# A graph-attention kernel: its general-path flag drawn in two steps, the last tile's stores on SP and GpSimd, and a last pass of 12 chunks

## The chip, the cores and the metric

The kernel runs on one core of one Trainium2 chip. A core has TensorE (PE, matrix products), VectorE (DVE), ScalarE (ACT), GpSimd (POOL) and SyncE (SP); each has its own instruction stream, they meet at semaphores, and 16 DMA engines move data between HBM and the on-chip memory. DMAs are issued here by SP, ACT and POOL. The metric is the time of one execution on the device in microseconds, the median of several.

## The reference, cut to what matters

One graph-attention layer over 4096 nodes with 128 features, then a residual and a layer norm:

```python
s_i = emb @ attn[:d]; s_j = emb @ attn[d:]          # emb is x, 4096 x 128
e = leaky_relu(s_i + s_j.T, negative_slope=0.2)
e = e + where(adj > 0, 0.0, -1e9)                   # adj is 4096 x 4096 int32
alpha = softmax(e, axis=1)
x = layernorm(x + alpha @ emb, axis=-1)
```

## The kernel before

**Main part.** The 4096 rows are 32 tiles of 128 rows, in 8 blocks of K = 4 tiles. The columns are 32 chunks of 128. For block n and chunk c, DVE makes one tile `weights` (128 x 512, line 674) out of row factors, column factors and the mask; PE then multiplies it, tile by tile, with `xj[:, c, 0:129]` (line 807; the 129th column gives the denominator) and sums over the chunks in four PSUM banks, one for each tile of the block. There are W_SLOTS = 12 buffers for `weights`: DVE may write chunk c once PE has used chunk c - 12 (semaphore `weights_used`). The adjacency comes in 32 pieces of 2 MB, half by SP's and half by ACT's DMAs; ACT turns them into bytes, DVE transposes those.

**The last pass.** In blocks 0 to 6 PE does the four tiles of each chunk in turn. In the last block it does this for the first CHUNKS - LAST chunks (LAST is 8) and then finishes tile after tile: 8 chunks of tile 0, 8 of tile 1, and so on (lines 827 to 835). After each of tiles 0 to 2 it raises `tile_summed`; the end of tile 3 is seen through `weights_used`.

**After the sums.** Tile 0 to tile 3 mean here the four tiles of the last block. They are handled in FINAL_GROUPS: tiles 0 and 1 together, tile 2, tile 3. For each group DVE clips the denominator (`denominators`, line 607), inverts it (`invert`, 613), forms y = sum/denominator + x (`add_x`, 619), and takes mean and variance (640 and 643). Group 0 is normalised by POOL (lines 324 to 331, reciprocal root) and ACT (465) and stored by POOL (4 DMAs of 32 KB, line 257 in `store_last`). For tiles 2 and 3 ACT takes the root of the variance (473), DVE inverts it (648) and normalises (651), raising `last_out_ready` to 1 and to 2; SP stores the partitions of quadrants 0 and 1 and ACT those of quadrants 2 and 3, two DMAs of 16 KB each for each tile (also `store_last`). SP and ACT issue tile 2's before tile 3's.

**The flag.** The fast computation holds only if no inverse of a denominator was very large. `worst` gathers the largest inverses (`largest_inverse`, line 625, after every block), DVE reduces it over its columns (666), PE turns the result into a row (839), DVE reduces the row (708) and compares it with MOST (710). The result is `again`, a number that every engine but POOL loads (`value_load`) to decide whether it jumps over the general path, a long piece of code of its own (lines 281 to 290, 487 and on, 713 and on, 842 and on). With the inputs used here it is 0, and all jump.

**The end.** Each engine goes to one last barrier (line 81, where the block of engine programs ends): a DRAIN, then a semaphore that POOL collects from all others before it lets them go. POOL gets there after it has waited for the landing of its own stores (`early_stored`), SP after its and ACT's stores (`last_stored`).

Of the kernel before, what the change touches and what calls it, by code (L numbers as in the profile page):

```python
# [9 lines left out]
def gat_kernel(nc: bass.Bass, x: bass.AP, adj: bass.AP, attn: bass.AP, out: bass.AP):  # L10
    fp32 = mybir.dt.float32
# [7 lines left out]
    P = 128  # L19
# [32 lines left out]
    LAST = 8  # L52
# [9 lines left out]
    MOST = 1e28  # L62
# [18 lines left out]
    with ExitStack() as ctx:  # L81
# [38 lines left out]
        worst = sb("worst", [P, T + 2], fp32)  # L120
# [69 lines left out]
        early_stored = sem("early_stored")  # L190
        last_stored = sem("last_stored")
# [6 lines left out]
        worst_turned = sem("worst_turned")  # L198
# [68 lines left out]
        @block.sync  # L267
        def _(sp):

            sp.dma_start(attn_row_in[:], attn[:, :].rearrange("d o -> o d")).then_inc(attn_loaded, 16)  # L270
            for part in range(X_PARTS):
                load_x(sp, LOW_HALF, part)
            for g in range(ALL_PIECES):
                load_piece(sp, LOW_HALF, g)


            for g in range(EARLY, len(FINAL_GROUPS)):
                sp.wait_ge(last_out_ready, g - EARLY + 1)
                for q in LOW_HALF:
                    store_last(sp, g, q, last_stored)  # L280


            sp.wait_ge(again_ready, 1)
            with sp.If(sp.value_load(again[0:1, 0:1], min_val=0, max_val=1) > 0):
                sp.wait_ge(stored, 16 * Q * NORM_GROUPS)
                sp.wait_ge(early_stored, 16 * Q * EARLY)
                sp.wait_ge(last_stored, 16 * Q * (len(FINAL_GROUPS) - EARLY))
                sp.dma_start(xi[:], xi_v).then_inc(inputs_again, 16)
                sp.dma_start(attn_col, attn[D:2 * D, :]).then_inc(inputs_again, 16)
                sp.dma_start(attn_row, attn[0:D, :].rearrange("d o -> o d").broadcast_to([P, D])).then_inc(inputs_again, 16)  # L290
                with sp.Fori(0, TILES) as t:
                    sp.wait_ge(adj_rows_free, t + 1)
                    sp.dma_start(adj_rows, adj[bass.ds(t * P, P), :]).then_inc(adj_rows_loaded, 16)
            sp.wait_ge(last_stored, 16 * Q * (len(FINAL_GROUPS) - EARLY))

        @block.gpsimd
        def _(pool):
# [34 lines left out]
            for g in range(EARLY):  # L332
                pool.wait_ge(early_out_ready, g + 1)
                for q in range(Q):
                    store_last(pool, g, q, early_stored)
            pool.wait_ge(early_stored, 16 * Q * EARLY)

        @block.scalar
        def _(act):
# [148 lines left out]
            with act.If(act.value_load(again[0:1, 0:1], min_val=0, max_val=1) > 0):  # L488
# [28 lines left out]
        def _(dve):  # L517
# [118 lines left out]
            def mean_and_variance(g):  # L636
                tiles = range(FINAL_GROUPS[g].start, FINAL_GROUPS[g].stop)
                for t in tiles:
                    dve.wait_ge(y_ready, FINAL + t + 1)
                    nc.vector.bn_stats(half_moments[:, t, :], tile(FINAL + t)).then_inc(half_moments_ready, 1)  # L640
                for t in tiles:
                    dve.wait_ge(half_moments_ready, t + 1)
                    nc.vector.bn_aggr(moments[:, t, :], half_moments[:, t, :]).then_inc(moments_ready, 1)  # L643
# [11 lines left out]
            def final_residual(n):  # L655

                for g in range(len(FINAL_GROUPS) + 1):
                    if g < len(FINAL_GROUPS):
                        denominators(n, g)
                        invert(n, g)  # L660
                        add_x(n, g)
                        mean_and_variance(g)
                    else:
                        largest_inverse(n)
                        dve.wait_ge(worst_ready, n + 2)
                        nc.vector.reduce_max(worst[:, T:T + 1], worst[:, 0:T], X).then_inc(worst_found, 1)
                    if g > EARLY:
                        last_normalise(g - 1)
# [45 lines left out]
            with dve.If(dve.value_load(again[0:1, 0:1], min_val=0, max_val=1) > 0):  # L714
# [41 lines left out]
        def _(pe):  # L756
# [81 lines left out]
            pe.wait_ge(worst_found, 1)  # L838
            nc.tensor.transpose(banks[0][0:1, 0:P], worst[:, T:T + 1], ident[:]).then_inc(worst_turned, 1)
# [3 lines left out]
            with pe.If(pe.value_load(again[0:1, 0:1], min_val=0, max_val=1) > 0):  # L843
# [51 lines left out]
```

## Time and profile before

| | us |
|---|---|
| median of 3 runs (lowest to highest) | 260.94 (260.23 to 261.37) |
| the profiled execution, its own time | 259.07 |
| its span (first to last instruction of the core) | 257.3 |
| outside the span, worked out | 1.8 |
| PE busy, DVE busy, ACT busy, POOL busy | 245.0, 235.3, 167.3, 37.4 |
| granted TensorE clock, mean | 0.994 |

The profile page gives busy time and shares over the whole span; the change touches only its last few microseconds, so that the view in order of time (start, duration, engine, line, tiles, count, and in brackets the idle time before and what ended it) is the one to read. The suffix q (PEldq, POOLq, SPq) stands for an engine's sequencer: branches, drains, register loads and DMA issues, which are not counted as busy. Such instructions are found by asking for one source line.

### The profile page before, as it was taken

How to read it: one execution, taken by the hardware profiler on the slowest of the kernel's cores; microseconds unless marked ns; L12 is line 12 of the kernel's file. 1: busy time of each engine (PE TensorE's matmuls, PEld its weight loads, DVE VectorE, ACT ScalarE, POOL GpSimd, SP SyncE). 2: the span in 40 equal slices, each digit the busy share in tenths (PEclk: the TensorE clock that was granted, in tenths of full speed). 3: DMA queues.
4: the chain of work that ended last, by engine and by line, in shares of the span. 5: the costliest groups of instructions: out<-in, count | busy, mean ns of one | idle time of the engine just before them, and what ended most of it. 6: DMA issues, size and time to landing. Idle time of an engine off the chain costs nothing.

```text
span 257.3 us, 5385 instructions
## 1 busy us (share of the span) xinstructions
PE 245.0 (95%) x2117; PEld 238.9 (93%) x2117; DVE 235.3 (91%) x384; ACT 167.3 (65%) x249; POOL 37.4 (15%) x74
## 2 busy tenths in 40 slices
PE   7888999999999999999999999999999999999980
PEld 6538999999999999999999999999999999999970
DVE  2979999999999999999999999999999999999252
ACT  2697999756875796569844985579653986053010
POOL 1000000000430123003300330034000320033022
PEclk9999999999999999999999999999999999999997
DMA  7999999999999999999999999999999990001001
GB/s 206 319 348 348 350 348 349 348 350 348 349 350 360 349 350 357 353 349 347 358 352 350 316 309 362 349 348 270 365 335 346 249 238 24 3 0 45 0 0 45
DMA packets 70237, 71.68 MB, mean 279 GB/s; under 512 B 2881, under 2 KB 68674, under 8 KB 70210
## 3 DMA queue, kind: packets, MB, share of 16 engines
q1 hardware_dynamic: 34594, 34.67, 44.1%
q10 hardware_dynamic: 34592, 34.67, 43.5%
q0 software_dynamic: 1024, 1.97, 2.3%
q8 instruction: 17, 0.28, 0.5%
q14 instruction: 10, 0.08, 0.1%
HBM read 69.21 MB, written 2.10 MB: 277 GB/s over the span
## 4 chain that ended last, share of the span: by engine, by line
PE 87%; DMA 5%; DVE 3%; SPq 1%; POOL 1%; issue 0%; ACT 0%; DVEq 0%; ACTq 0%
PE psum L807 87%; DMA adj_in<-in_adj_dram 5%; DVE weights L674 1%; SPq L232 1%; DVE mask_bytes L583 1%; POOL out_dram L257 1%; DVE mask_t L578 1%; ACT x_raw L465 0%; SPq L249 0%; DVE x_raw L619 0%; SPq L270 0%; DVE half_moments L640 0%; ACT deviations L473 0%; DVE moments L643 0%; DVE rden L613 0%
## 5 line engine op out<-in xcount | busy, mean ns | idle before, releaser
L807 PEld LDWEIGHTS psum<-xj,weights 128*128 128x128 f32 x2048 | 229.0, 192 | 2.8 <-ACT xj L373 1.7
L807 PE MATMUL psum<-xj,weights 128*128 128x129 f32 x2048 | 229.3, 275 | 1.8 <-DVE weights L674 0.9
L674 DVE SCALAR_TENSOR_TENSOR weights<-q_row,r_j,mask_t 128x512 f32<-128x512 f32 x256 | 172.6, 739 | 1.7
L390 ACT ACTIVATE mask_bytes<-adj_in 128x4096 uint8<-128x4096 int32 x27 | 97.5, 3611 | 30.3 <-DMA adj_in<-in_adj_dram 30.3
L565 DVE STREAM_TRANSPOSE mask_t<-mask_bytes 128x1024 uint32<-128x1024 uint32 x27 | 33.4, 1236 | 0.5 <-ACT mask_bytes L390 0.5
L310 POOL TENSOR_SCALAR neg_mean<-total 128x4 f32<-128x4 f32 x7 | 3.9, 560 | 166.7 <-ACT x_raw L396 166.7
L396 ACT ACTIVATE x_raw<-x_raw 128x128 f32<-128x128 f32 x28 | 8.3, 297 | 21.2 <-DVE x_raw L619 21.2
L319 POOL DMA_DIRECT2D out_dram<-x_raw x28 | 14.6, 526 | 20.0 <-ACT x_raw L410 20.0
L384 ACT ACTIVATE mask_bytes<-adj_in 128x2048 uint8<-128x2048 int32 x8 | 15.1, 1901 | 1.7 <-DMA adj_in<-in_adj_dram 1.7
L403 ACT ACTIVATE unused<-x_raw,neg_mean 128x128 f32<-128x128 f32 x28 | 10.9, 390 | 4.8 <-POOL neg_mean L310 4.8
L410 ACT ACTIVATE x_raw<-x_raw,offset,rstd 128x128 f32<-128x128 f32 x28 | 11.5, 480 | 2.3 <-POOL offset L316 2.3
L473 ACT ACTIVATE deviations<-moments,eps 128x1 f32<-128x1 f32 x2 | 0.6, 294 | 15.8 <-DVE moments L643 15.8
L373 ACT ACTIVATE xj<-x_raw,d_j 128x128 f32<-128x128 f32 x32 | 10.1, 392 | 0.0
L314 POOL TENSOR_TENSOR rstd<-variance,half 128x4 f32<-128x4 f32 x7 | 10.0, 1423 | 0.6
L619 DVE SCALAR_TENSOR_TENSOR x_raw<-psum,rden,x_raw 128x128 f32<-128x128 f32 x32 | 9.2, 345 | 0.4
L607 DVE TENSOR_SCALAR rden<-psum 128x4 f32<-128x4 f32 (+2 forms) x10 | 1.5, 154 | 7.1 <-PE psum L807 7.1
L785 PE MATMUL psum<-adj_in,attn_iw 128*128 128x512 f32 x16 | 7.5, 594 | 0.0
L578 DVE STREAM_TRANSPOSE mask_t<-mask_bytes 128x512 uint32<-128x512 uint32 x10 | 7.1, 706 | 0.1
L774 PEld LDWEIGHTS psum<-ident,x_raw 128*128 128x128 f32 x32 | 3.5, 140 | 2.9 <-DMA x_raw<-in_x_dram 2.2
L346 ACT COPY adj_in<-psum 128x512 f32<-128x512 f32 x8 | 4.4, 582 | 2.5 <-PE psum L774 1.7
L774 PE MATMUL psum<-ident,x_raw 128*128 128x128 f32 x32 | 4.3, 278 | 1.2 <-DMA x_raw<-in_x_dram 1.2
L396 ACT ACTIVATION_READ_ACCUMULATOR x_raw<-x_raw 128x1 f32 x28 | 5.2, 187 | 0.0
(58 smaller groups left out, 58.0 us busy)
## 6 DMA issues: line engine op xcount, KB each, us to landing
adj_in<-in_adj_dram ACTq DMA_DIRECT2D x64, 512.0 KB, 13.4
adj_in<-in_adj_dram SPq DMA_DIRECT2D x64, 512.0 KB, 14.0
out_dram<-x_raw POOLq DMA_DIRECT2D x28, 64.0 KB, 5.3
x_raw<-in_x_dram ACTq DMA_DIRECT2D x4, 128.0 KB, 3.1
x_raw<-in_x_dram SPq DMA_DIRECT2D x4, 128.0 KB, 3.4
x_raw<-in_x_dram ACTq DMA_DIRECT2D x2, 256.0 KB, 5.9
x_raw<-in_x_dram SPq DMA_DIRECT2D x2, 256.0 KB, 6.5
out_dram<-x_raw POOLq DMA_DIRECT2D x4, 32.0 KB, 1.8
```

The lines of the kernel that those rows point to most:

```text
L314: nc.gpsimd.tensor_tensor(rstd[:, 0:K], variance[:, 0:K], half[:, 0:K], ALU.pow).then_inc(rstd_ready, 1)
L319: pool.dma_start(out_v[g, q, :, :], x_raw[B * q:B * (q + 1), g * K:(g + 1) * K, :].rearrange("b k d -> b (k d)")).then_inc(stored, 16)
L373: nc.scalar.activation(xj[:, c, 0:D], x_raw[:, c, :], ACT.Copy, scale=d_j[:, c:c + 1]).then_inc(xj_scaled, 1)
L384: half_bytes = nc.scalar.activation(mask_bytes[:, g % BYTE_SLOTS, :, :, part], adj_in[:, g % ADJ_SLOTS, :, :, part], ACT.Sign)
L390: nc.scalar.activation(mask_bytes[:, g % BYTE_SLOTS, :, :, :], adj_in[:, g % ADJ_SLOTS, :, :, :], ACT.Sign).then_inc(bytes_ready, 1)
L396: last = nc.scalar.activation(tile(g * K + k), tile(g * K + k), ACT.Identity, accum_out=total[:, k:k + 1])
L403: last = nc.scalar.activation(unused[:, k, :], tile(g * K + k), ACT.Square, bias=neg_mean[:, k:k + 1], accum_out=square_sum[:, k:k + 1])
L410: last = nc.scalar.activation(tile(g * K + k), tile(g * K + k), ACT.Identity, bias=offset[:, k:k + 1], scale=rstd[:, k:k + 1])
L565: nc.vector.transpose(dst.rearrange("p f (r a) -> p r f a", a=B), src).then_inc(mask_ready, 1)
L578: nc.vector.transpose(dst.rearrange("p (r a) -> p r a", a=B), src).then_inc(mask_ready if f else half_mask_ready, 1)
L674: nc.vector.scalar_tensor_tensor(weights[:, slot_of(n, c), :], q_row[:, n * BANK:(n + 1) * BANK], r_j[:, c:c + 1], mask_t[:, (n * PIECES + ...
L807: return nc.tensor.matmul(banks[(n * K + t) % 8][:, 0:D1], weights[:, slot_of(n, c), t * P:(t + 1) * P], xj[:, c, 0:D1], start=(c == 0), s ...
```

## The change

- `LAST` goes from 8 to 12.
- `largest_inverse` no longer ends the last block. The gathered `worst`, with the inverses of all tiles but the last, is reduced and scaled to `risk[:, 0]` ahead of the last tile's sums; the last tile's inverse is taken into `risk[:, 1]` by one more instruction; PE turns `risk[:, 1]`; one reduction writes `again` directly, as an integer, between the last tile's statistics and their aggregation. The comparison with MOST is gone: a scale by 0.5e-28 and the conversion to an integer stand for it.
- ACT normalises group 0 before it takes tile 2's root, and stores its half of tile 2 before it takes tile 3's root. POOL stores ACT's half of tile 3 and waits for it before the last barrier.
- The last statistics are split into `statistics` and `mean_and_variance` (same instructions).

```diff
-    LAST = 8
+    LAST = 12
...
-    MOST = 1e28
+    SHARE_OF_MOST = 0.5e-28
...
@@ SP @@
             for g in range(EARLY, len(FINAL_GROUPS)):
                 sp.wait_ge(last_out_ready, g - EARLY + 1)
                 for q in LOW_HALF:
-                    store_last(sp, g, q, last_stored)
+                    store_last(sp, g, q, stored_by_queues)
...
-            sp.wait_ge(last_stored, 16 * Q * (len(FINAL_GROUPS) - EARLY))
+            sp.wait_ge(stored_by_queues, 16 * (Q + len(LOW_HALF)))
@@ POOL @@
-                    store_last(pool, g, q, early_stored)
-            pool.wait_ge(early_stored, 16 * Q * EARLY)
+                    store_last(pool, g, q, stored_by_pool)
+            pool.wait_ge(last_out_ready, 2)
+            for q in HIGH_HALF:
+                store_last(pool, EARLY + 1, q, stored_by_pool)
+            pool.wait_ge(stored_by_pool, 16 * (Q + len(HIGH_HALF)))
@@ ACT @@
-            for g in range(EARLY - 1):
-                last_normalise(g)
+            last_normalise(0)
             last_deviations(EARLY)
-            last_normalise(EARLY - 1)
+            act.wait_ge(last_out_ready, 1)
+            for q in HIGH_HALF:
+                store_last(act, EARLY, q, stored_by_queues)
             last_deviations(EARLY + 1)
-            for g in range(EARLY, len(FINAL_GROUPS)):
-                act.wait_ge(last_out_ready, g - EARLY + 1)
-                for q in HIGH_HALF:
-                    store_last(act, g, q, last_stored)
@@ DVE, final_residual @@
-                for g in range(len(FINAL_GROUPS) + 1):
-                    if g < len(FINAL_GROUPS):
-                        denominators(n, g)
-                        invert(n, g)
-                        add_x(n, g)
-                        mean_and_variance(g)
-                    else:
-                        largest_inverse(n)
-                        dve.wait_ge(worst_ready, n + 2)
-                        nc.vector.reduce_max(worst[:, T:T + 1], worst[:, 0:T], X).then_inc(worst_found, 1)
-                    if g > EARLY:
-                        last_normalise(g - 1)
+                for g in range(EARLY + 1):
+                    denominators(n, g)
+                    invert(n, g)
+                    add_x(n, g)
+                    statistics(g)
+                    mean_and_variance(g)
+                last_normalise(EARLY)
+                dve.wait_ge(worst_ready, n + 1)
+                nc.vector.tensor_tensor(worst[:, 0:T], worst[:, 0:T], rden[:], ALU.max).then_inc(worst_ready, 1)
+                dve.wait_ge(worst_ready, n + 2)
+                nc.vector.reduce_max(worst[:, T:T + 1], worst[:, 0:T], X).then_inc(worst_found, 1)
+                dve.wait_ge(worst_found, 1)
+                nc.vector.tensor_scalar(risk[:, 0:1], worst[:, T:T + 1], SHARE_OF_MOST, None, ALU.mult).then_inc(risk_known, 1)
+
+                g = EARLY + 1
+                denominators(n, g)
+                invert(n, g)
+                dve.wait_ge(rden_ready, n + g + 1)
+                dve.wait_ge(risk_known, 1)
+                nc.vector.scalar_tensor_tensor(risk[:, 1:2], rden[:, K - 1:K], SHARE_OF_MOST, risk[:, 0:1],
+                                               ALU.mult, ALU.max).then_inc(risk_known, 1)
+                add_x(n, g)
+                statistics(g)
+                dve.wait_ge(risk_turned, 1)
+                nc.vector.reduce_max(again[:], banks[0][0:1, 0:P], X).then_inc(again_ready, 1)
+                mean_and_variance(g)
+                last_normalise(g)
...
-            dve.wait_ge(worst_turned, 1)
-            nc.vector.reduce_max(worst[0:1, T + 1:T + 2], banks[0][0:1, 0:P], X).then_inc(worst_found, 1)
-            dve.wait_ge(worst_found, 2)
-            nc.vector.tensor_scalar(again[:], worst[0:1, T + 1:T + 2], MOST, None, ALU.is_gt).then_inc(again_ready, 1)
@@ PE @@
-            pe.wait_ge(worst_found, 1)
-            nc.tensor.transpose(banks[0][0:1, 0:P], worst[:, T:T + 1], ident[:]).then_inc(worst_turned, 1)
+            pe.wait_ge(risk_known, 2)
+            nc.tensor.transpose(banks[0][0:1, 0:P], risk[:, 1:2], ident[:]).then_inc(risk_turned, 1)
```

The end of DVE's program before, from the inversion of tile 3's denominator to the flag (in brackets the semaphores that an instruction waits for):

```order
L613 RECIPROCAL rden<-rden 128x1 [waits den_ready]
L619 SCALAR_TENSOR_TENSOR x_raw<-psum,rden,x_raw 128x128 [waits rden_ready]
L640 BN_STATS half_moments<-x_raw 128x6 [waits y_ready]
L643 BN_AGGR moments<-half_moments 128x2 [waits half_moments_ready]
L648 RECIPROCAL rstd<-deviations 128x1 [waits last_deviation_ready]
L651 TENSOR_SCALAR x_raw<-x_raw,moments,rstd 128x128 [waits last_rstd_ready]
L625 TENSOR_TENSOR worst<-worst,rden 128x8 [waits worst_ready,rden_ready]
L666 TENSOR_REDUCE worst<-worst 128x1 [waits worst_ready]
L648 RECIPROCAL rstd<-deviations 128x1 [waits last_deviation_ready]
L651 TENSOR_SCALAR x_raw<-x_raw,moments,rstd 128x128 [waits last_rstd_ready]
L708 TENSOR_REDUCE worst<-psum 1x1 [waits worst_turned]
L710 TENSOR_SCALAR again<-worst 1x1 [waits worst_found]
```

And now, from the normalisation of tile 2 to the aggregation of tile 3's statistics (L651 and L654, tile 3's own normalisation, follow):

```order
L651 RECIPROCAL rstd<-deviations 128x1 [waits last_deviation_ready]
L654 TENSOR_SCALAR x_raw<-x_raw,moments,rstd 128x128 [waits last_rstd_ready]
L668 TENSOR_TENSOR worst<-worst,rden 128x8 [waits worst_ready]
L670 TENSOR_REDUCE worst<-worst 128x1 [waits worst_ready]
L672 TENSOR_SCALAR risk<-worst 128x1 [waits worst_found]
L609 TENSOR_SCALAR rden<-psum 128x1 [waits weights_used]
L615 RECIPROCAL rden<-rden 128x1 [waits den_ready]
L679 SCALAR_TENSOR_TENSOR risk<-rden,risk 128x1 [waits risk_known,rden_ready]
L621 SCALAR_TENSOR_TENSOR x_raw<-psum,rden,x_raw 128x128 [waits rden_ready]
L641 BN_STATS half_moments<-x_raw 128x6 [waits y_ready]
L684 TENSOR_REDUCE again<-psum 1x1 [waits risk_turned]
L646 BN_AGGR moments<-half_moments 128x2 [waits half_moments_ready]
```

Tile 2's normalisation and the gathering of `worst` now stand ahead of tile 3's denominator; behind it the flag needs one instruction of 128 x 1 and one reduction, and the reduction stands ahead of tile 3's aggregation.

ACT's last instructions before, from tile 2's root to the last DMA issue:

```order
L473 ACTIVATE deviations<-moments,eps 128x1 [waits moments_ready,last_deviation_ready]
L465 ACTIVATE x_raw<-x_raw,offset,rstd 128x128 [waits offset_ready]
L465 ACTIVATE x_raw<-x_raw,offset,rstd 128x128
L473 ACTIVATE deviations<-moments,eps 128x1 [waits moments_ready]
L257 DMA out_dram<-x_raw 32x128 [waits last_out_ready]
L257 DMA out_dram<-x_raw 32x128
L257 DMA out_dram<-x_raw 32x128 [waits last_out_ready]
L257 DMA out_dram<-x_raw 32x128
```

And now:

```order
L470 ACTIVATE x_raw<-x_raw,offset,rstd 128x128 [waits offset_ready,last_deviation_ready]
L470 ACTIVATE x_raw<-x_raw,offset,rstd 128x128
L478 ACTIVATE deviations<-moments,eps 128x1 [waits moments_ready]
L259 DMA out_dram<-x_raw 32x128 [waits last_out_ready]
L259 DMA out_dram<-x_raw 32x128
L478 ACTIVATE deviations<-moments,eps 128x1 [waits moments_ready]
```

Two of ACT's four issues are gone, and the other two stand ahead of tile 3's root.

POOL's last instructions now, from group 0's variance to the end; the two DMAs of 32x128 are new, all else was there before:

```order
L326 TENSOR_SCALAR variance<-moments 128x2 [waits moments_ready]
L328 TENSOR_SCALAR neg_mean<-moments 128x2
L331 TENSOR_TENSOR rstd<-variance,half 128x2 [waits variance_ready]
L333 TENSOR_TENSOR offset<-neg_mean,rstd 128x2 [waits rstd_ready]
L259 DMA out_dram<-x_raw 32x256 [waits early_out_ready]
L259 DMA out_dram<-x_raw 32x256 x3
L259 DMA out_dram<-x_raw 32x128 [waits last_out_ready]
L259 DMA out_dram<-x_raw 32x128
L81 UNCONDITIONAL_BRANCH [waits stored_by_pool]
```

The branch to the last barrier now waits for tile 3's stores, where it waited for group 0's alone.

## Rows read from the trace of the kernel before

**Rows 1.** In order of time, last 20 us: start us, us, engine line, tiles, count [idle before].

```profile
237.83 11.78 PE L807 MATMUL psum<-xj,weights 128*128 128x129 f32 x104
...
238.03 1.64 DVE L674 SCALAR_TENSOR_TENSOR weights<-q_row,r_j,mask_t 128x512 f32<-128x512 f32 x2
246.07 0.16 DVE L607 TENSOR_SCALAR rden<-psum 128x2 f32<-128x2 f32 x1 [6.40 <-PE psum L807]
...
247.86 0.16 DVE L607 TENSOR_SCALAR rden<-psum 128x1 f32<-128x1 f32 x1 [0.17 <-PE psum L807]
...
249.44 0.86 ACT L465 ACTIVATE x_raw<-x_raw,offset,rstd 128x128 f32<-128x128 f32 x2
249.65 0.16 DVE L607 TENSOR_SCALAR rden<-psum 128x1 f32<-128x1 f32 x1 [0.50 <-PE psum L807]
...
250.42 0.29 DVE L640 BATCH_NORM_STATS2 half_moments<-x_raw 128x6 f32<-128x128 f32 x1
250.60 2.07 POOL L257 DMA_DIRECT2D out_dram<-x_raw  x4 [1.30 <-ACT x_raw L465]
250.75 0.18 DVE L643 BATCH_NORM_AGGREGATE moments<-half_moments 128x2 f32<-128x6 f32 x1
...
250.97 0.29 ACT L473 ACTIVATE deviations<-moments,eps 128x1 f32<-128x1 f32 x1 [0.66 <-DVE moments L643]
...
251.28 0.16 DVE L625 TENSOR_TENSOR worst<-worst,rden 128x8 f32<-128x8 f32 x1
251.39 1.75 SPq L257 DMA_DIRECT2D out_dram<-x_raw  x4
...
251.47 0.16 DVE L666 TENSOR_REDUCE worst<-worst 128x1 f32<-128x8 f32 x1
251.55 0.15 DVE L648 RECIPROCAL rstd<-deviations 128x1 f32<-128x1 f32 x1
...
251.69 0.27 PE L839 MATMUL psum<-ident,worst 128*1 128x128 f32 x1 [2.08 <-DVE worst L666]
251.74 0.34 DVE L651 TENSOR_SCALAR x_raw<-x_raw,moments,rstd 128x128 f32<-128x128 f32 x1
252.00 0.27 DVE L708 TENSOR_REDUCE worst<-psum 1x1 f32<-1x128 f32 x1
252.31 0.14 DVE L710 TENSOR_SCALAR again<-worst 1x1 int32<-1x1 f32 x1
```

**Rows 2.** Line 843, PE's jump over the general path: ns min/median/max, first and last start.

```profile
L843 PEldq TENSOR_LOAD <-again x1: 502/502/502, 252.5 to 252.5; - x1
...
L843 PEldq COMPARE_BRANCH  x1: 3374/3374/3374, 253.4 to 253.4; - x1
```

**Rows 3.** Line 714, DVE's jump over the general path.

```profile
L714 DVEq COMPARE_BRANCH  x1: 72/72/72, 253.4 to 253.4; - x1
```

**Rows 4.** Line 81, the last barrier.

```profile
L81 POOLq COMPARE_BRANCH  x1: 33/33/33, 254.2 to 254.2; - x1
L81 POOLq DRAIN  x1: 2674/2674/2674, 254.4 to 254.4; - x1
...
L81 SPq DRAIN  x1: 7/7/7, 255.3 to 255.3; - x1
L81 PEldq DRAIN  x1: 73/73/73, 256.8 to 256.8; - x1
```

**Rows 5.** Line 885, the barrier at the start of the program.

```profile
L885 POOLq DRAIN  x1: 169/169/169, 0.3 to 0.3; - x1
```

**Rows 6.** DMA issues from 225 us on: count, KB each, median us to landing.

```profile
out_dram<-x_raw POOLq DMA_DIRECT2D x4, 32.0 KB, 1.8
out_dram<-x_raw SPq DMA_DIRECT2D x4, 16.0 KB, 2.0
```

**Rows 7.** DMA queues between 255 and 256 us: packets, MB, share.

```profile
q14 instruction: 1, 0.01, 3.1%
```

More of the change, by code:

```diff
@@ L117, in gat_kernel @@
         eps = sb("eps", [P, 1], fp32)
-        worst = sb("worst", [P, T + 2], fp32)
+        worst = sb("worst", [P, T + 1], fp32)
+        risk = sb("risk", [P, 2], fp32)
         again = sb("again", [1, 1], i32)
@@ L189, in gat_kernel @@
         last_out_ready = sem("last_out_ready")
-        early_stored = sem("early_stored")
-        last_stored = sem("last_stored")
+        stored_by_pool = sem("stored_by_pool")
+        stored_by_queues = sem("stored_by_queues")
         variance_ready = sem("variance_ready")
@@ L197, in gat_kernel @@
         worst_ready = sem("worst_ready")
-        worst_turned = sem("worst_turned")
+        risk_known = sem("risk_known")
+        risk_turned = sem("risk_turned")
         worst_found = sem("worst_found")
@@ L279, in _ @@
                 for q in LOW_HALF:
-                    store_last(sp, g, q, last_stored)
+                    store_last(sp, g, q, stored_by_queues)
             sp.wait_ge(again_ready, 1)
-            with sp.If(sp.value_load(again[0:1, 0:1], min_val=0, max_val=1) > 0):
+            with sp.If(sp.value_load(again[0:1, 0:1], min_val=0, max_val=2 ** 30) > 0):
                 sp.wait_ge(stored, 16 * Q * NORM_GROUPS)
-                sp.wait_ge(early_stored, 16 * Q * EARLY)
-                sp.wait_ge(last_stored, 16 * Q * (len(FINAL_GROUPS) - EARLY))
+                sp.wait_ge(stored_by_pool, 16 * (Q + len(HIGH_HALF)))
+                sp.wait_ge(stored_by_queues, 16 * (Q + len(LOW_HALF)))
                 sp.dma_start(xi[:], xi_v).then_inc(inputs_again, 16)
@@ L293, in _ @@
                     sp.dma_start(adj_rows, adj[bass.ds(t * P, P), :]).then_inc(adj_rows_loaded, 16)
-            sp.wait_ge(last_stored, 16 * Q * (len(FINAL_GROUPS) - EARLY))
+            sp.wait_ge(stored_by_queues, 16 * (Q + len(LOW_HALF)))
         @block.gpsimd
@@ L473, in last_deviations @@
                 nc.scalar.activation(deviations[:, v], moments[:, v, 1], ACT.Sqrt, bias=eps[:]).then_inc(last_deviation_ready, 1)
-            for g in range(EARLY - 1):
-                last_normalise(g)
+            last_normalise(0)
             last_deviations(EARLY)
-            last_normalise(EARLY - 1)
+            act.wait_ge(last_out_ready, 1)
+            for q in HIGH_HALF:
+                store_last(act, EARLY, q, stored_by_queues)
             last_deviations(EARLY + 1)
-            for g in range(EARLY, len(FINAL_GROUPS)):
-                act.wait_ge(last_out_ready, g - EARLY + 1)
-                for q in HIGH_HALF:
-                    store_last(act, g, q, last_stored)
             act.wait_ge(stored, 16 * Q * NORM_GROUPS)
             act.wait_ge(again_ready, 1)
-            with act.If(act.value_load(again[0:1, 0:1], min_val=0, max_val=1) > 0):
+            with act.If(act.value_load(again[0:1, 0:1], min_val=0, max_val=2 ** 30) > 0):
                 for m in range(TILES // 4):
@@ L634, in residual, with statistics, mean_and_variance @@
                 largest_inverse(n)
-            def mean_and_variance(g):
-                tiles = range(FINAL_GROUPS[g].start, FINAL_GROUPS[g].stop)
-                for t in tiles:
+            def statistics(g):
+                for t in range(FINAL_GROUPS[g].start, FINAL_GROUPS[g].stop):
                     dve.wait_ge(y_ready, FINAL + t + 1)
                     nc.vector.bn_stats(half_moments[:, t, :], tile(FINAL + t)).then_inc(half_moments_ready, 1)
-                for t in tiles:
+            def mean_and_variance(g):
+                for t in range(FINAL_GROUPS[g].start, FINAL_GROUPS[g].stop):
                     dve.wait_ge(half_moments_ready, t + 1)
@@ L704, in _ @@
             final_residual(BLOCKS - 1)
-            dve.wait_ge(worst_turned, 1)
-            nc.vector.reduce_max(worst[0:1, T + 1:T + 2], banks[0][0:1, 0:P], X).then_inc(worst_found, 1)
-            dve.wait_ge(worst_found, 2)
-            nc.vector.tensor_scalar(again[:], worst[0:1, T + 1:T + 2], MOST, None, ALU.is_gt).then_inc(again_ready, 1)
             dve.wait_ge(again_ready, 1)
-            with dve.If(dve.value_load(again[0:1, 0:1], min_val=0, max_val=1) > 0):
+            with dve.If(dve.value_load(again[0:1, 0:1], min_val=0, max_val=2 ** 30) > 0):
                 dve.wait_ge(inputs_again, 48)
@@ L835, in _ @@
                     last.then_inc(tile_summed, 1)
-            pe.wait_ge(worst_found, 1)
-            nc.tensor.transpose(banks[0][0:1, 0:P], worst[:, T:T + 1], ident[:]).then_inc(worst_turned, 1)
+            pe.wait_ge(risk_known, 2)
+            nc.tensor.transpose(banks[0][0:1, 0:P], risk[:, 1:2], ident[:]).then_inc(risk_turned, 1)
             pe.wait_ge(again_ready, 1)
-            with pe.If(pe.value_load(again[0:1, 0:1], min_val=0, max_val=1) > 0):
+            with pe.If(pe.value_load(again[0:1, 0:1], min_val=0, max_val=2 ** 30) > 0):
                 pe.wait_ge(inputs_again, 48)
```

## The prediction

> **What bounds the kernel now.** I read first the page's shares: PE is busy for nearly the whole span, and the chain of waits is PE's products for almost all of it. So only two things can matter: something that makes PE's last product later, or something between that product and the end. The view in order of time gives the first point: PE multiplies without a gap to about 249.6 us, and DVE sees the last tile at 249.65 [rows 1]. From there to the end of the span, 257.3 us, are 7.6 us without any product, and that is where the change works. The chain as printed ends with POOL's stores of group 0, and stops short of the real end, since it leaves sequencers out. So I asked for the lines of the jumps and of the last barrier. Two engines come last, close together. PE: the flag is written at 252.31 + 0.14 = 252.45 us [rows 1], PE loads it at 252.5, starts its jump at 253.4, and the jump takes 3.37 us [rows 2], while DVE's takes 0.07 [rows 3]; PE is at the barrier at 256.8 + 0.07 = 256.9 us [rows 4]. POOL: its four stores are issued from 250.60 to 252.67 us [rows 1], the last begins about 252.2 and has landed when POOL branches at 254.2; then its DRAIN begins at 254.4 and takes 2.67 us, to 257.07 [rows 4]. POOL is thus the last by 0.2 us, PE the second; SP, with the stores of tile 3, is there at 255.3 [rows 4] and has 1.8 us to spare. This is the picture on which everything below rests: two floors 0.2 us apart, one made by the flag and one by POOL's stores. The change lowers the first and raises the second.
>
> **LAST from 8 to 12.** 104 records in 11.78 us are 0.113 us each, two to a product, so a product is 0.225 us [rows 1]; tiles follow each other by 8 products, 1.8 us (246.07, 247.86, 249.65). With 12 they follow by 12 x 0.225 = 2.7 us. The number of products is the same, so tile 3 ends at the same 249.6, tile 2 at 246.95 (0.9 earlier) and tiles 0 and 1 at 244.25 (1.8 earlier). What could be lost is DVE's lead: PE now needs chunk 31's weights for tile 0 at 249.6 - 48 x 0.225 + 11 x 0.225 = 241.3 us; DVE has written them at 238.03 + 1.64 = 239.67. The buffer for chunk 31 comes free with chunk 19 in both orders, so DVE is no earlier or later. 1.6 us are left and the edit costs nothing on PE's path. It only moves group 0 and tile 2.
>
> **Group 0 and tile 2.** ACT's normalisation of group 0 goes from 249.44 to about 247.6; it is now ahead of tile 2's root, which has its variance at about 248.3, so neither waits long. POOL stores group 0 from 250.60 - 1.9 = 248.7 to 250.8 and is free again 1.3 us before tile 3 is ready. DVE normalises tile 2 at about 248.8 to 249.15, and the three instructions on `worst` and `risk` start 0.19 us apart (251.28 to 251.47, [rows 1]): 249.1, 249.3, 249.5. They end within 0.05 us of the moment when tile 3's sum is there; I put 0 to 0.1 us, and take 0.
>
> **The flag.** Denominator at 249.65, inverse 0.2 later, the new `risk` instruction 0.2 later at 250.04, where `add_x` stood; `add_x` and the statistics slip by the distance between two instructions that do not wait for each other, 0.1 us, so the statistics begin at 250.52 instead of 250.42. PE's turn starts 0.22 us after its source's start and the reduction 0.31 us after that (251.47, 251.69, 252.00 [rows 1]): 250.04 + 0.22 + 0.31 = 250.57, which is before the statistics are done. So the reduction starts at about 250.8 and the flag is there at 251.05: 1.4 us earlier than 252.45. PE's barrier time becomes 256.9 - 1.4 = 255.5 us.
>
> **Tile 3.** The reduction (0.27) stands ahead of the aggregation: that goes from 250.75 to about 251.05. The root follows 0.22 behind, ends at 251.56, the inverse at 251.6 and the normalisation from 251.8 to 252.14. Before, it ended at 251.74 + 0.34 = 252.08: the root was done at 251.26, but the inverse began only at 251.55, as two instructions on `worst` stood ahead of it [rows 1]. Taking those away pays for the reduction put in. Net 0.06 later, with ends of -0.15 and +0.3. The wait for the turned row holds up exactly this chain, BN_AGGR first, and through it the root and all stores. ACT's two issues for tile 2, 0.9 us from about 249.2, are over long before the root at 251.27.
>
> **The stores of tile 3.** SP's two go from second place behind tile 2's to an idle queue; it gains some 0.1 us from it, then loads the flag, and is at the barrier near 254.8. POOL's two are the point. POOL starts 0.3 us after what it waits for (ACT's end at 249.44 + 0.86 = 250.30, POOL at 250.60), each issue takes 0.52 us (2.07 for four): first at 252.4, second at 252.95. Landing: POOL's 32 KB take a median of 1.8 us and the last one took 2.0 (252.2 to 254.2), SP's 16 KB take 2.0 [rows 1, 4, 6]. No row has a 16 KB store of POOL. From below: start 0.05 us after the wait and 1.8 us of flight, landing at 254.5; from above: 2.3 us of flight, 255.3. I take 1.9, between POOL's own values: 254.85, against 254.2 now. Then come the branch, 0.15 us, and the DRAIN, 2.67 us: 257.7 us.
>
> By the Trainium skill (DMA: Bandwidth & Descriptors, Specifications) a DMA issued by GpSimd has a first-byte latency of about 1 us against 0.6 us for one of SP or ACT, which speaks against giving POOL the last store. The rows do not show it: POOL's stores of twice the size landed no later than SP's. By that rule the landing would be an estimated 0.4 us later still; I do not add it.
>
> **The sum.** Of the profiled execution: end now set by POOL at 257.07, then by POOL at 257.7, PE at 255.5, SP at 254.8. That is +0.6 us; with the ends above +0.3 to +1.1. I take +0.55: span 257.85, and time 259.07 + 0.55 = 259.6. The profiled execution is 1.9 us below the median of the runs shown, for reasons that do not lie in the tail; so the same step on the median gives 260.94 + 0.55 = 261.5.
>
> **Rivals.** (a) POOL's long DRAIN is not tied to its stores. For it: the same DRAIN at the program's start takes 0.17 us [rows 5], and it ends within 0.2 us of PE's arrival, which could be more than chance. Also, one packet of instructions was fetched in that stretch, between 255 and 256 us [rows 7], 1 us or so behind POOL's branch, and PE's long jump is of the same length, about 3 us, where DVE's short one is nothing. Then the DRAIN's length belongs to where POOL's code lies, and the code is three instructions longer now. Against it: PE's time stands on its jump, POOL's on its DRAIN, after a branch of only 33 ns, and at the program's start there were no stores behind the DRAIN. If the 2.7 us are gone, POOL is ready at about 255.1, PE's 255.5 sets the end, and the time is 1.4 to 1.6 us less than before: 259.5 us. The Trainium skill (Runtime: NRT & Kernel Launch, Instruction fetch mechanics) says that a taken branch out of the two pages held makes the engine fetch the target's page first; PE's row agrees with that, and for POOL it would give this rival. Another page of it (Perfetto Trace Analysis, Per-instruction lifecycle) says that a sequencer instruction's window opens when its semaphore waits are over; by that the 2.67 us are not a wait for PE.
>
> (b) Slower, at PE: DVE's lead is too short. In the last pass PE uses a chunk every 0.225 us, and DVE makes one in 0.75 (1.64 for two with a wait between). If chunk 31's weights come more than 1.6 us later than in this trace, PE stops, and each further microsecond costs one. An execution whose adjacency lands 3 us later would cost 1.4 us on top of the 0.55: 262.9. Against it: DVE was waiting for a free buffer for its last two chunks, so that its lead was at its full 12 slots.
>
> (c) Slower, small: the turned row comes late (PE's first instruction after a pause) and holds BN_AGGR by another 0.3 to 0.5 us; all stores slip by it: 261.9. It decides only beyond the 0.25 us that the statistics cover.
>
> (d) The wait for `weights` or the flag changes nothing that is seen: POOL and PE both keep the end within 0.2 us: 260.9. That is the low end of my own case.
>
> **Chances.** Forecast, POOL's DRAIN behind its later stores: 0.66, with (d) in it, 260.9 to 262.1 by itself. (a) 0.24 at 259.5. (b) 0.04, (c) 0.06. A measurement of this kernel can tell about 0.5%, 1.3 us, from no change. (a) lies at -0.55%, just over this bound, and gives a little over half of its chance to faster, 0.14, the rest to no change; (b), half of (c) and the upper tail of my own case give slower 0.08; no change 0.78. The range from 259.3 to 262.2 takes in (a), my case and (c).
>
> **What would show it.** Each step has its place in the view in order of time: denominators of tiles 0 and 1 at 244.3 and of tile 2 at 247, tile 3's still at 249.65 (else (b)); the flag's reduction at 250.8, followed at once by BN_AGGR (else (c)); the last normalisation ending near 252.1; POOL's last store issued near 252.95. In the rows of the barrier PE's DRAIN stands at 255.4 and POOL's begins near 255.0 and takes 2.7 us. If that DRAIN is short or begins as late and ends at PE's time, I am wrong and (a) is right.

## The result

The changed kernel takes 261.12 us (median of 20 runs), the kernel before 259.68 (median of 20 runs too; the three shown ahead, median 260.94, are among its six slowest). The ratio is 1.0043, 95% interval 1.0029 to 1.0056: 1.1 us slower (the two medians lie 1.4 us apart). The ratios here and below leave out three slow executions, one of the kernel before at 380.04 us and two of e7 at 264.99 and 273.40 us. The forecast was 0.55 us slower and "no change" within 0.5%; the direction and the mechanism hold, and the forecast size is half of the measured one. That its absolute 261.5 lies near 261.12 is luck: the base was taken too high by 1.26 us and the step too low. On the base of 259.68 the same steps give 260.2 us and a range that ends at 260.9, 0.2 us below the median that was measured.

The two profiled executions differ by 2.6 us in span (257.3 and 259.9), but 1.0 of this is ahead of the tail: the products ended at 249.6 before and at 250.6 now, with the change not yet reached. So everything below is told from the end of the products (row L819: 237.80 + 12.79 = 250.59; before 237.83 + 11.78 = 249.61, [rows 1]); a number with a plus sign is a time in us after that end. From there to the end of the span are 7.7 us before and 9.3 now.

The tail after, in order of time:

```profile
237.80 12.79 PE L819 MATMUL psum<-xj,weights 128*128 128x129 f32 x113
...
245.26 0.16 DVE L609 TENSOR_SCALAR rden<-psum 128x2 f32<-128x2 f32 x1 [4.61 <-PE psum L819]
...
250.53 0.15 DVE L672 TENSOR_SCALAR risk<-worst 128x1 f32<-128x1 f32 x1
250.62 0.16 DVE L609 TENSOR_SCALAR rden<-psum 128x1 f32<-128x1 f32 x1
...
251.68 0.26 DVE L684 TENSOR_REDUCE again<-psum 1x1 int32<-1x128 f32 x1
251.87 0.16 DVE L646 BATCH_NORM_AGGREGATE moments<-half_moments 128x2 f32<-128x6 f32 x1
...
252.59 0.35 DVE L654 TENSOR_SCALAR x_raw<-x_raw,moments,rstd 128x128 f32<-128x128 f32 x1
253.23 0.98 POOL L259 DMA_DIRECT2D out_dram<-x_raw  x2 [1.41 <-DVE x_raw L654]
```

Against [rows 1]: tile 3's denominator is touched at +0.03 us after the products (before +0.04), so the work put ahead of it costs nothing; the flag is written at +1.35 (before +2.84); tile 3 is normalised at +2.35 (before +2.47). All this is as good as or better than forecast. POOL's last store is issued about half a microsecond after 253.23, at +3.1, where its last was issued at about +2.6.

The last barrier (line 81) after, against [rows 4]:

```profile
L81 PEldq DRAIN  x1: 73/73/73, 256.6 to 256.6; - x1
L81 SPq DRAIN  x1: 7/7/7, 256.7 to 256.7; - x1
L81 POOLq COMPARE_BRANCH  x1: 33/33/33, 256.7 to 256.7; - x1
L81 POOLq DRAIN  x1: 2837/2837/2837, 256.8 to 256.8; - x1
```

PE's jump before that barrier (line 855) took:

```profile
L855 PEldq COMPARE_BRANCH  x1: 3657/3657/3657, 252.9 to 252.9; - x1
```

PE is at the barrier at +6.1 us instead of +7.3, but POOL branches at +6.1 instead of +4.6, and its DRAIN now takes 2.84 us instead of 2.67. The sum: 1.5 + 0.16 = 1.6 us longer, all of it POOL's. POOL's branch waits for the landing of its last store, and that flight took 2.9 us where 1.9 was forecast. What happened in it, from the DMA queues between 253.9 and 255.15 us, and behind that between 255.15 and 257:

```profile
DMA packets 119, 0.06 MB, mean 46 GB/s; under 512 B 51, under 2 KB 118, under 8 KB 118
...
q0 software_dynamic: 60, 0.03, 10.9%
q1 hardware_dynamic: 58, 0.02, 6.0%
...
out_dram<-x_raw POOLq DMA_DIRECT2D x1, 16.0 KB, 2.9
```

```profile
DMA packets 10, 0.00 MB, mean 2 GB/s; under 512 B 4, under 2 KB 10, under 8 KB 10
...
q1 hardware_dynamic: 6, 0.00, 1.3%
q0 software_dynamic: 4, 0.00, 0.8%
```

Nearly all packets have started by 255.15; ten stragglers, 4 of POOL's queue (q0) and 6 of SP's (q1), move only later. Beside them lies one packet of 16 KB on q8, which I take for the instructions that PE fetches for its jump (e3, without the jump, has none there). Between 253.6 and 257 us:

```profile
q8 instruction: 1, 0.02, 2.3%
...
out_dram<-x_raw SPq DMA_DIRECT2D x1, 16.0 KB, 3.2
```

By the records of single packets it began at 253.90 and ended at 255.17 (2.3% of 16 engines' 3.4 us is 1.25 us), and the first straggler started at 255.17. SP's last store took 3.2 us to land.

### The profile page after: what moved, and what is told of

The parts are those of the page before. It is cut to its first block, busy times and chain, and to the rows that moved or that the text cites. A ratio compares the mean times of both kernels' runs of the same rounds, so it can differ in the third digit from the quotient of the medians.

```text
span 259.9 us, 5386 instructions
## 1 busy us (share of the span) xinstructions
PE 246.0 (95%) x2117; PEld 239.9 (92%) x2117; DVE 235.8 (91%) x385; ACT 167.3 (64%) x249; POOL 37.5 (14%) x76
## 3 DMA queue, kind: packets, MB, share of 16 engines
q0 software_dynamic: 1088, 2.00, 2.3%
## 4 chain that ended last, share of the span: by engine, by line
PE 87%; DVE 5%; DMA 2%; ACT 2%; POOL 1%; issue 1%; SPq 1%; ACTq 0%; DVEq 0%
PE psum L819 85%; DMA x_raw<-in_x_dram 2%; DVE weights L692 1%; PE psum L786 1%; DVE mask_bytes L585 1%; PE psum L797 1%; ACT adj_in L360 1%; DVE mask_t L580 1%; SPq L234 0%; POOL out_dram L259 0%; DVE x_raw L621 0%; ACT x_raw L470 0%; POOL rstd L331 0%; DVE x_raw L654 0%; DVE half_moments L641 0%
## 5 line engine op out<-in xcount | busy, mean ns | idle before, releaser
L819 PEld LDWEIGHTS psum<-xj,weights 128*128 128x128 f32 x2048 | 229.0, 192 | 2.0 <-issue 2.0
L819 PE MATMUL psum<-xj,weights 128*128 128x129 f32 x2048 | 229.3, 275 | 1.0 <-DVE weights L692 0.9
L415 ACT ACTIVATE x_raw<-x_raw,offset,rstd 128x128 f32<-128x128 f32 x28 | 11.5, 479 | 2.3 <-POOL offset L318 2.3
L470 ACT ACTIVATE x_raw<-x_raw,offset,rstd 128x128 f32<-128x128 f32 x2 | 0.9, 486 | 13.5 <-POOL offset L333 13.5
L797 PE MATMUL psum<-adj_in,attn_iw 128*128 128x512 f32 x16 | 8.1, 629 | 0.0
L786 PEld LDWEIGHTS psum<-ident,x_raw 128*128 128x128 f32 x32 | 4.3, 161 | 3.5 <-DMA x_raw<-in_x_dram 2.3
L786 PE MATMUL psum<-ident,x_raw 128*128 128x128 f32 x32 | 5.1, 313 | 2.1 <-DMA x_raw<-in_x_dram 2.1
L528 DVE TENSOR_TENSOR adj_in<-x_raw,attn_j 128x1024 f32<-128x1024 f32 x4 | 4.8, 1221 | 0.9 <-DMA x_raw<-in_x_dram 0.9
```

The source lines that it names most:

```text
L415: last = nc.scalar.activation(tile(g * K + k), tile(g * K + k), ACT.Identity, bias=offset[:, k:k + 1], scale=rstd[:, k:k + 1])
L786: last = nc.tensor.transpose(banks[XT_BANK + m % 4][:, k * P:(k + 1) * P], x_raw[:, m * K + k, :], ident[:])
L797: nc.tensor.matmul(banks[bank][:, :], attn_iw[:], xT[:, rb * BANK:(rb + 1) * BANK], start=True, stop=True).then_inc(s_i_in_psum, 1)
L819: return nc.tensor.matmul(banks[(n * K + t) % 8][:, 0:D1], weights[:, slot_of(n, c), t * P:(t + 1) * P], xj[:, c, 0:D1], start=(c == 0), s ...
```

## The experiments

Times are set against the kernel before, run beside it on the same chip. "Tail" is the span's end less the end of the products in the profiled execution; before it is 7.7 us. The tail is that of one execution: its difference to 7.7 us and the step of the timed runs agree only within about 1 us (3.1 against 2.1 us in e2, 1.6 against 1.1 in the changed kernel).

| run | ratio (95%) | tail us | DRAIN of POOL us | POOL DMAs in the program |
|---|---|---|---|---|
| changed kernel | 1.0043 (1.0029 to 1.0056) | 9.3 | 2.837 | 34 |
| e1, ACT stores | 0.9947 (0.9928 to 0.9966) | 6.7 | 2.674 | 32 |
| e2, POOL's stores alone | 1.0082 (1.0063 to 1.0102) | 10.8 | 2.837 | 34 |
| e3, no jump of PE | 1.0024 (1.0008 to 1.0041) | 8.4 | 2.837 | 34 |
| e4, SP awaits POOL's stores | 0.9999 (0.9988 to 1.0009) | 8.0 | 4.711 | 34 |
| e5, LAST = 12 alone | 1.0002 (0.9991 to 1.0014) | 7.8 | 2.674 | 32 |
| e6, e1 with LAST = 8 | 1.0017 (1.0007 to 1.0027) | 8.4 | 2.674 | 32 |
| e7, one POOL DMA a block | 1.0006 (0.9994 to 1.0018) | 7.7 | 1.131 | 13 |
| e8, e1 with whole-tile stores | 0.9949 (0.9935 to 0.9963) | 6.0 | 2.674 | 32 |
| e9, e1 again | 0.9947 (0.9931 to 0.9962) | 6.7 | 2.674 | 32 |
| e10, e8 again | 0.9935 (0.9917 to 0.9953) | 6.2 | 2.674 | 32 |
| e11, e8 and e7 together | 0.9960 (0.9937 to 0.9983) | 6.0 | 0.967 | 11 |
| e12, before, one POOL DMA a block | 1.0008 (0.9994 to 1.0022) | 7.5 | 0.967 | 11 |

**e1, tile 3's upper half back on ACT.**

```diff
 # ACT, after tile 3's root
+            act.wait_ge(last_out_ready, 2)
+            for q in HIGH_HALF:
+                store_last(act, EARLY + 1, q, stored_by_queues)
 # POOL
-            pool.wait_ge(last_out_ready, 2)
-            for q in HIGH_HALF:
-                store_last(pool, EARLY + 1, q, stored_by_pool)
-            pool.wait_ge(stored_by_pool, 16 * (Q + len(HIGH_HALF)))
+            pool.wait_ge(stored_by_pool, 16 * Q)
```

SP's last wait counts ACT's two stores as well.

> The changed kernel, but tile 3's upper half is stored by ACT again (behind its root), so that POOL issues and awaits nothing after group 0. Theory A (the end is the landing of POOL's last store plus a DRAIN of 2.7 to 2.8 us): POOL's DRAIN begins some 3 us after the end of PE's products instead of 6.2, ends before PE's jump does, and PE or SP sets the end; time 0.9 to 1.4% below the changed kernel, ratio to before 0.990 to 0.996. The stores of SP and ACT still land about 3 us after their issue if the fetch behind PE's jump delays them. Rival B (the loss of the changed kernel lies elsewhere, in a later end of the products or in the flag's instructions on DVE): ratio to before stays near 1.004. Rival C (the DRAIN waits for PE, not for stores): POOL's DRAIN would end at PE's arrival, and be shorter or longer than 2.7 us by that.

Ratio 0.9947: 2.5 us below the changed kernel, and 1.4 below the kernel before. The barrier's rows of e1:

```profile
L81 POOLq DRAIN  x1: 2674/2674/2674, 252.3 to 252.3; - x1
...
L81 SPq COMPARE_BRANCH  x1: 38/38/38, 256.0 to 256.0; - x1
L81 PEldq DRAIN  x1: 72/72/72, 256.0 to 256.0; - x1
```

POOL's DRAIN has the length of before and is over at 255.0, one microsecond before PE arrives: it follows POOL's stores and not PE (rival C falls, rival B too). PE and SP now end together. The stragglers are there again, six of SP's queue and six of ACT's (q10), from 254.4 to 255.5 us:

```profile
q1 hardware_dynamic: 6, 0.00, 1.9%
q10 hardware_dynamic: 6, 0.00, 1.8%
```

The first of them started within 0.02 us of the end of PE's 16 KB packet, and so it is in every trace in which stores of 16 KB were in flight behind that packet: the changed kernel, e1, e2, e4, e6, e7 and e9.

**e2, the kernel before with POOL's stores of tile 3.**

```diff
-            pool.wait_ge(early_stored, 16 * Q * EARLY)
+            pool.wait_ge(last_out_ready, 2)
+            for q in HIGH_HALF:
+                store_last(pool, EARLY + 1, q, early_stored)
+            pool.wait_ge(early_stored, 16 * (Q + len(HIGH_HALF)))
 # ACT stores only tile 2's upper half
```

> The kernel before with one edit: POOL stores tile 3's upper half. LAST is 8 and the flag is as late as before, so PE's jump and its instruction fetch (16 KB in one packet of about 1 us) come after most of the stores. Theory A1 (the fetch delays the last landing): POOL's second store lands 1.9 to 2.2 us after its issue, ratio to before 1.002 to 1.004, POOL last with DRAIN of about 2.8 us. Rival D (a 16 KB store of POOL takes 3 us by itself): landing 2.9 us after the issue and ratio 1.005 to 1.007.

A miss for A1 as stated, by its size: 2.1 us slower, more than the whole change. The flag is late here, but so is POOL's store, behind group 0's four; it was issued at +3.55 us, landed 4.0 us later, and POOL's branch came at +7.6. Two of its packets moved when the fetch for PE's jump ended, at 256.6 us (packets from 256.6 on):

```profile
DMA packets 2, 0.00 MB, mean 1 GB/s; under 512 B 1, under 2 KB 2, under 8 KB 2
## 3 DMA queue, kind: packets, MB, share of 16 engines
q0 software_dynamic: 2, 0.00, 0.7%
```

So the late flag did not keep the fetch out of the way; it put the fetch on the last store's final packets, which is worse. PE's packet ran from +5.5 to +6.5 us, and one of 8 KB on q14 (1.1 us after ACT's jump) from +4.8 to +5.2; how much of the delay of those two packets is due to each is not shown. The ratio is above what rival D forecast too (POOL's 16 KB are slow by themselves, 1.005 to 1.007), though its interval reaches there; e3 decides.

**e3, PE without the general path.** The lines from `pe.wait_ge(again_ready, 1)` to the end of PE's program are left out.

> The changed kernel without the general path on PE: PE neither loads the flag nor jumps (that path could not run; its work on PE is left out). Theory A1: no 16 KB fetch in the middle of tile 3's stores, POOL's last store lands 1.9 to 2.1 us after its issue instead of 2.9, the DRAIN still takes 2.8 us, and the time is about 1 us below the changed kernel: ratio to before 0.999 to 1.001. Rival D (POOL's small store is slow by itself): landing and time stay as in the changed kernel, ratio 1.004.

DMA issues from 252.3 us on, and POOL at the barrier:

```profile
out_dram<-x_raw POOLq DMA_DIRECT2D x2, 16.0 KB, 2.0
out_dram<-x_raw SPq DMA_DIRECT2D x1, 16.0 KB, 2.2
```

```profile
L81 POOLq COMPARE_BRANCH  x1: 33/33/33, 254.5 to 254.5; - x1
L81 POOLq DRAIN  x1: 2837/2837/2837, 254.7 to 254.7; - x1
```

Same stores, issued at the same distance from the products; without the jump they land after 2.0 and 2.2 us instead of 2.9 and 3.2, and the tail is 0.9 us shorter. Rival D falls. The 8 KB packet of q14 is still there (0.56 us from +3.45), so that it alone does not delay them. In the timed runs the gain over the changed kernel is 0.5 us (1.0043 to 1.0024, on two chips, with intervals that overlap), less than the 1 us expected; whether the collision costs less in most executions than in the profiled one is not shown. What is left against the kernel before is 0.6 us, which is what the prediction forecast (0.55) without the collision.

**e4, SP waits for POOL's stores.** One line, `wait_ge(stored_by_pool, 16 * (Q + len(HIGH_HALF)))`, goes from the end of POOL's program to the end of SP's.

> The changed kernel with one line moved: the wait for the landing of POOL's stores stands on SP instead of POOL. Theory A with a DRAIN of fixed length: POOL's DRAIN starts when its last issue is done, 3.6 us after the products' end instead of 6.2, and ends at about the time PE and SP arrive; the time falls by 2 to 2.7 us against the changed kernel, ratio to before 0.993 to 0.997. Rival E (the DRAIN itself waits until the stores have landed and are accounted for): it begins earlier, lasts 5 us, and the time stays: ratio 1.004. Rival C (DRAIN waits for PE): it ends with PE's arrival.

```profile
L81 POOLq DRAIN  x1: 4711/4711/4711, 253.3 to 253.3; - x1
...
L81 PEldq DRAIN  x1: 73/73/73, 256.5 to 256.5; - x1
L81 SPq COMPARE_BRANCH  x1: 38/38/38, 256.6 to 256.6; - x1
```

Between the two theories: the DRAIN begins 3.2 us earlier and is 1.9 us longer. It ends 1.4 us after the landing that SP waits for, where it ended 3.0 after it when POOL waited first. Its record begins just before POOL's last DMA is issued (+3.05 us against +3.13), so that this issue of 0.5 us and the flight lie in it. About half of the usual 2.84 us overlaps with the flight. What exactly it waits for in the other half stays open. The time falls by 1.1 us, to that of before.

**e5, LAST = 12 alone; e6, the early flag without it.** e5 is the kernel before with `LAST = 12`, e6 is e1 with `LAST = 8`.

> The kernel before with LAST = 12 and nothing else. ACT takes tile 2's root first, so group 0 is normalised only 0.9 us earlier, POOL's stores land 0.9 us earlier and its DRAIN (2.67 us) ends at 256.2 instead of 257.1 in the time of the trace of before; the flag and PE's jump stay where they are, PE at 256.9. Theory A (two floors, PE 0.2 us under POOL): the time falls by 0.2 us at most, ratio 0.998 to 1.000. Rival F (a longer last pass costs something of its own, in DVE's lead or in PE): ratio over 1.001 and a gap in PE's products.

> The kernel of e1 (early flag, ACT stores) with LAST = 8 again. DVE must normalise tile 2 and gather the flag before it may touch tile 3, and ACT does group 0 first: tile 3's denominator begins some 1.5 us after the end of the products instead of 0.05 us, the flag at +2.9 us, the last stores 1.5 us later than in e1. Theory A: PE and SP at the barrier 1.5 us later than in e1, ratio to before 1.000 to 1.004. Rival G (LAST = 12 is of no use to the flag, since DVE has time anyway): ratio as e1, 0.995.

Both as expected within their intervals. e5 is worth nothing by itself: POOL's DRAIN is over at +6.3 us, and PE, at +7.5, sets the end. In e6 DVE waits for tile 2's root and comes late to tile 3:

```profile
250.51 0.16 DVE L651 RECIPROCAL rstd<-deviations 128x1 f32<-128x1 f32 x1 [1.33 <-ACT deviations L475]
...
251.43 0.15 DVE L609 TENSOR_SCALAR rden<-psum 128x1 f32<-128x1 f32 x1
```

That is +1.8 us after the products' end at 249.63, where e1 has +0.04; e6 is 1.8 us slower than e1. LAST = 12 is what makes room for the early flag.

**e7, fewer DMAs of POOL.** The changed kernel, with

```diff
-                for q in range(Q):
-                    pool.dma_start(out_v[g, q, :, :],
-                                   x_raw[B * q:B * (q + 1), g * K:(g + 1) * K, :].rearrange("b k d -> b (k d)")).then_inc(stored, 16)
+                pool.dma_start(out_v[g, :, :, :],
+                               x_raw[:, g * K:(g + 1) * K, :].rearrange("p k d -> p (k d)")).then_inc(stored, 16)
```

> The changed kernel, but POOL stores each of blocks 0 to 6 with one DMA of 256 KB instead of four of 64 KB: POOL issues 13 DMAs in the whole program instead of 34. The DRAIN took 2.674 us after 32 DMAs and 2.837 after 34, that is 0.08 us for each and almost nothing besides. Theory H (the DRAIN's length is 0.08 us for each DMA that POOL has issued in the program): 1.1 to 1.2 us, POOL's end 1.7 us earlier than in the changed kernel, so that PE, SP and POOL come within 0.5 us: ratio to before 0.996 to 0.999. Rival J (the DRAIN has a fixed length of about 2.7 us): 2.7 to 2.85 us and ratio 1.004.

```profile
L81 POOLq COMPARE_BRANCH  x1: 33/33/33, 256.2 to 256.2; - x1
L81 POOLq DRAIN  x1: 1131/1131/1131, 256.4 to 256.4; - x1
```

Theory H holds: 13, 32 and 34 DMAs give 1.131, 2.674 and 2.837 us, which is 0.075 + 0.081 for each. It is the number of DMAs and not what they carry: the bytes on POOL's queue (q0) are 2.0 MB in both kernels, its packets are 2096 here and 1088 in the changed kernel, and POOL's other instructions are the same. The tail falls by 1.6 us, as expected, but the time by 1.0 us and not by 1.7, in part because more of it now lies outside the span: 2.05 us (median of its runs) instead of 1.8; e11 and e12, which have the same edit, show it too (2.0 and 2.1), and in all three traces one more instruction packet of 8 KB is fetched after the span.

**e8 to e10, tile 2 and tile 3 each in one DMA.** e1, with ACT's store of tile 2 and SP's of tile 3 as one DMA of 64 KB over 128 partitions.

> The kernel of e1, but tile 2 is stored by ACT in one DMA of 64 KB and tile 3 by SP in one: the last issue begins 2.4 us after the end of the products instead of 2.8. Theory A1 (what lands last in e1 is what shares a DMA engine with the instruction fetch behind PE's jump): the store's data are mostly out before the fetch starts at +3.3 us, landing at +4.6 to +5.2 instead of +6.3, the fetch is less disturbed and PE's jump takes 3.4 to 3.7 us instead of 4.0; PE sets the end at +5.8 to +6.1 and the ratio to before is 0.992 to 0.994. Rival K (a DMA over 128 partitions is slower to land, or the fetch still delays it): ratio as e1 or above, 0.995.

> The same kernel as e1, beside e10 on the same chip. In e1's trace a few packets of the last stores moved only after the instruction fetch behind PE's jump had ended, and the last store landed at +6.3 us after the products. Theory A1: the same again; ratio to before 0.993 to 0.996. It is here to be compared with e10.

> The same kernel as e8, beside e9 on the same chip. Its trace had a tail 0.7 us shorter than e1's (5.98 against 6.68 us after the products), but the two times, from different chips, did not show it. Theory A1: about 0.5 us under e9, ratio to before 0.991 to 0.994. Rival K (the shorter tail was that one execution's, and whole-tile stores are worth nothing): as e9 within 0.2 us.

The trace of e8 shows the times that were expected: SP's branch at 255.2 us, +5.1 instead of e1's +6.3, and PE's jump of 3.35 us instead of 3.97, PE last:

```profile
L81 SPq DRAIN  x1: 7/7/7, 255.4 to 255.4; - x1
L81 PEldq DRAIN  x1: 73/73/73, 255.8 to 255.8; - x1
```

The reason given beforehand fails, though. The store's packets were not out before the fetch: PE's 16 KB packet began at +3.3 us and the store's first at +3.7, its last at +4.7, and about two thirds of them moved while the fetch was on. Why this store lands sooner than those of e1 stays open. And side by side (e9, e10) the ratios are 0.9947 and 0.9935 with overlapping intervals: 0.3 us is seen of the 0.5 to 0.7 us by which the tails differ. Inconclusive as a gain; either version beats both kernels.

**e11, e8 with e7's edit; e12, the kernel before with e7's edit.**

> e10 with one POOL DMA for each of blocks 0 to 6, so that POOL issues 11 in the program. Theory H: DRAIN of 0.97 us (0.075 + 0.081 x 11), POOL at the barrier 1.7 us earlier than in e10, where PE's jump is the last already: the time is e10's within 0.3 us. Rival L (POOL's end or its descriptor work still costs something there): 0.5 us or more under e10.

> The kernel before with one POOL DMA for each of blocks 0 to 6 (11 in the program) and nothing else. Theory H with two floors 0.2 us apart: DRAIN of 0.97 us, POOL ready at +5.8 us after the products instead of +7.5, PE's jump sets the end at +7.3: ratio to before 0.998 to 1.000. Rival J (the DRAIN has a fixed length): no change at all and a DRAIN of 2.7 us. If the time fell by over 0.5%, POOL alone had set the end and PE's jump had not been close behind.

The DRAIN takes 0.967 us in both, the 0.97 worked out beforehand, and neither is faster for it (e11 at 0.9960 is not below e10's 0.9935): PE's jump sets the end (in e12 PE is at the barrier at 258.0 + 0.07 us, POOL's DRAIN is over at 256.6). In e12 the tail is 0.2 us shorter and the part outside the span 0.3 longer. With POOL 1.7 us earlier at the barrier PE still sets the end: this shows the floor that PE makes in the kernel before.

```profile
L81 POOLq DRAIN  x1: 967/967/967, 255.6 to 255.6; - x1
...
L81 PEldq DRAIN  x1: 73/73/73, 258.0 to 258.0; - x1
```

## Why the prediction held, and where its size was off

- **Two floors, one lowered, one raised: right.** PE's floor fell by 1.2 us (forecast 1.4; the flag came 1.5 earlier, but the jump was 0.3 longer), POOL's rose by 1.6 (forecast 0.6). e5 and e12 lowered POOL's floor alone and gained nothing; e1 lowered both, for 1.4 us. That lowering PE's alone would bring 0.2 us at most is read from the trace, and no run tested it.
- **LAST = 12 costs nothing: right**; denominators at 245.26 for tiles 0 and 1 (-5.3 us from the products' end, forecast -5.35), no gap in the products. Rival (b) fell.
- **The flag and tile 3's chain: right**, within 0.2 us (the flag written at +1.35 where +1.44 was forecast, tile 3 normalised at +2.35 where +2.53 was, POOL's last issue at +3.1 where +3.35 was); the turned row was there in time, and rival (c) fell.
- **"Landing ... I take 1.9": mis-sized.** It was 2.9 us. It makes the error of the sum: POOL's end came 1.0 us later than forecast, +1.0 for the flight, +0.16 for the DRAIN and -0.2 for the issue. The row used (POOL's stores before the jump) was from a time when no instructions were fetched. The upper bound of 2.3 was too low as well. The forecast moved the flag 1.4 us earlier without asking what else moves with it: the 16 KB fetch behind PE's jump, which had begun after the last data packets and now began before the last stores' (the fetch at +3.3 us, POOL's packets of tile 3 from +3.7 to +5.0). e3 shows PE's jump with its fetch as the cause, for 0.9 us in the trace and 0.5 in the timed runs. SP's stores met it too: SP was at the barrier at +6.1 us where +5.2 was forecast. The Trainium skill (DMA: Bandwidth & Descriptors, Specifications) gives a first-byte latency of about 1 us for GpSimd's DMAs against 0.6 us for those of SP and ACT. This is not what it was: with no fetch the 16 KB landed after 2.0 us from POOL and 2.2 from SP.
- **"the DRAIN, 2.67 us": slightly low**, since it grows with every DMA that POOL has issued: 0.16 us for two. The base too: see the result.
- **Rival (a), a DRAIN not tied to the stores: wrong.** With POOL's stores landed it kept its length wherever it began (e1, e3), and its end 0.2 us from PE's arrival was chance: in e1 they are 1.0 us apart. The instruction packet that spoke for it is ACT's: it came 1.1 us after ACT's branch over the general path in the traces before, after and of e1, wherever POOL's branch was. The Trainium skill (Runtime: NRT & Kernel Launch, Instruction fetch mechanics) says that a taken branch to a target outside the two pages held makes the engine fetch that page first. PE's jump agrees with it (a 16 KB packet 1.05 us after the branch began), and in e1 and e3 no such packet comes at that distance behind POOL's branch, while the DRAIN has its full length.

## What to carry to other kernels

When two engines arrive at the last barrier within 0.2 us of each other, an edit that speeds up one of them is worth no more than that, and one that slows the other down is paid in full: list every engine's arrival, sequencer rows included, before moving work between them. The end of GpSimd's program cost here a DRAIN that grew by 0.08 us with every DMA it had issued in the whole program, behind the last landing that it waited for: let it finish early. PE's jump over a long piece of code brought a fetch of 16 KB, and small stores in flight landed about 1 us later for it, so see what is in flight when it comes.

## What the runs showed of the hardware

- GpSimd's DRAIN at the end: 0.967, 1.131, 2.674 and 2.837 us after 11, 13, 32 and 34 DMAs; 4.711 us when it begins before the last has landed. At the program's start, with none issued, it took 0.169 us [rows 5].
- A jump of PE over the general path took 3.35 to 4.08 us; with stores of 16 KB in flight it was at the long end (3.66 and 3.69 in the changed kernel and e7, 3.91 to 4.08 in e4, e6, e1, e9 and e2), with one whole-tile store or none 3.35 to 3.63. The ranges nearly meet, so that a delay of the jump by the stores is likely and not shown.
- Stores of 16 KB in flight behind PE's fetch of 16 KB had 2 to 12 packets left that started when the fetch ended (seven traces); without the jump (e3) there were none, and the last landings were 0.9 us earlier. Whether they share a DMA engine with the fetch the records do not say.
- With three instructions for each of seven blocks fewer on GpSimd (e7, e11, e12), 0.2 to 0.3 us more passed outside the span.
